# Load order at the start of a fused cross-attention and FFN kernel: three batches of x and context ahead of scales, zeros and packed weights, with one GpSimd reduction and one row maximum moved

## The reference, cut to what matters

```python
def xattn(up, down, Wq, Wk, Wv, Wskip):           # up = layernorm(x)
    q, k, v = Wq @ up, Wk @ down, Wv @ down        # per batch
    attention = softmax(q.T @ k / sqrt(128), axis=-1)      # 1024 x 256
    return Wskip @ up + v @ attention.T

x = x + xattn(layernorm(x), ctx, Wq, Wk, Wv, Wskip)
Wg, Wu, Wd = (dequantize(W_q, scale, zero) for gate, up, down)   # int4, groups of 64
n = layernorm(x)
x = x + (silu(n @ Wg.T) * (n @ Wu.T)) @ Wd.T      # 1024 -> 2752 -> 1024, 2048 tokens
```

## Time and profile before

| | us |
|---|---|
| median of 3 runs | 1503.36 |
| lowest and highest of them | 1502.53, 1504.96 |
| the profiled execution, its own time | 1508.22 |
| span of its instructions | 1506.3 |
| PE busy (share of the span) | 1456.6 (97%) |
| VectorE busy | 797.2 (53%) |
| ScalarE busy | 656.0 (44%) |
| GpSimd busy | 220.6 (15%) |
| mean granted TensorE clock, of full speed | 0.992 |

### The profile page before, as it was taken

How to read it: one execution, slowest core, us unless ns; L and a number is a source line. 1 busy time by engine, 2 the same in 40 slices (tenths; PEclk the granted TensorE clock), 3 DMA queues, 4 the chain that set the end, 5 groups by cost and what they waited for, 6 DMA issues and landing times.

```text
span 1506.3 us, 18670 instructions
## 1 busy us (share of the span) xinstructions
PE 1456.6 (97%) x6774; PEld 716.0 (48%) x6774; DVE 797.2 (53%) x1143; ACT 656.0 (44%) x1221; POOL 220.6 (15%) x281
## 2 busy tenths in 40 slices
PE   5999999999999999999999999999999999999995
PEld 4666665444444444444444444444444444444442
DVE  4788887745544544544544554553554554553330
ACT  4888884244244343333333433433433334334343
POOL 0223231011011111111111101101101101101112
PEclk8999999999999999999999999999999999999999
DMA  5222222157547647648638638638638637638739
GB/s 147 95 95 91 82 88 70 43 92 148 110 75 162 111 70 167 111 64 173 111 57 179 111 56 177 116 48 174 116 54 168 115 64 156 122 62 165 140 67 168
DMA packets 44723, 166.42 MB, mean 110 GB/s; under 512 B 6416, under 2 KB 9232, under 8 KB 40336
## 3 DMA queue, kind: packets, MB, share of 16 engines
q0 software_dynamic: 25344, 92.29, 37.1%
q1 hardware_dynamic: 19200, 73.42, 17.6%
q10 hardware_dynamic: 144, 0.26, 0.0%
HBM read 65.28 MB, written 100.66 MB: 110 GB/s over the span
## 4 chain that ended last, share of the span: by engine, by line
PE 88%; DVE 5%; issue 3%; ACT 2%; DMA 1%; POOL 0%; POOLq 0%; ACTq 0%; DVEq 0%
PE ps L487 47%; PE ps L543 26%; PE ps L449 3%; PE ps L416 3%; PE ps L444 2%; PE ps L633 2%; PE ps L438 2%; PE ps L404 1%; PE ps L648 1%; DVE w_gu L1106 1%; DVE neg_max L1029 1%; ACT stage L797 1%; DMA out<-stage 1%; ACT temps L686 1%; DVE quant L1122 0%
## 5 line engine op out<-in xcount | busy, mean ns | idle before, releaser
L487 PE MATMUL ps<-xt,w_gu 128*128 128x512 f16 x3528 | 790.9, 380 | 2.2 <-ACT temps L767 2.2
L487 PEld LDWEIGHTS ps<-xt,w_gu 128*128 128x128 f16 x3528 | 345.5, 98 | 418.6 <-ACT temps L767 3.0
L543 PE MATMUL ps<-w_d_all,h_all 128*128 128x512 f16 x1920 | 440.6, 379 | 5.6 <-ACT stage L797 5.6
L797 ACT ACTIVATE stage<-ps,pow 128x512 f32<-128x512 f32 x352 | 240.5, 687 | 407.1 <-PE ps L543 390.3
L364 POOL DMA_DIRECT2D out<-stage x176 | 152.4, 866 | 1098.4 <-ACT stage L797 1098.4
L543 PEld LDWEIGHTS ps<-w_d_all,h_all 128*128 128x128 f16 (+1 forms) x1920 | 187.2, 98 | 234.4 <-ACT stage L797 10.1
L1170 DVE TENSOR_TENSOR temps<-ps,temps 128x512 f32<-128x512 f32 x42 | 29.0, 692 | 237.7 <-PE ps L487 237.7
L784 ACT CAST h_all<-temps 128x512 f16<-128x512 f32 x42 | 25.8, 613 | 132.4 <-DVE temps L1189 132.4
L1175 DVE TENSOR_TENSOR temps<-ps,temps 128x512 f32<-128x512 f32 x42 | 29.0, 691 | 95.4 <-PE ps L487 95.4
L1179 DVE TENSOR_TENSOR temps<-ps,temps 128x512 f32<-128x512 f32 x42 | 28.9, 689 | 75.8 <-PE ps L487 75.8
L1183 DVE TENSOR_TENSOR temps<-ps,temps 128x512 f32<-128x512 f32 x42 | 28.9, 689 | 75.1 <-PE ps L487 75.1
(11 more groups left out here) (112 smaller groups left out, 1262.4 us busy)
## 6 DMA issues: line engine op xcount, KB each, us to landing
out<-stage POOLq DMA_DIRECT2D x176, 512.0 KB, 5.4
grid<-grids SPq DMA_DIRECT2D x136, 256.0 KB, 4.9
raw<-packed SPq DMA_DIRECT2D x22, 512.0 KB, 4.2
stage<-x SPq DMA_DIRECT2D x13, 512.0 KB, 3.9
out<-stage SPq DMA_DIRECT2D x13, 512.0 KB, 2.9
raw_d<-packed SPq DMA_DIRECT2D x12, 512.0 KB, 7.9
w_gu<-ctx SPq DMA_DIRECT2D x16, 128.0 KB, 2.0
w_gu<-x SPq DMA_DIRECT2D x3, 512.0 KB, 3.4
```

Of the source, the lines that this page charges most:

```text
L487: mm = pe.matmul(bank, w_gu[e][:, wp, w, P * j:P * j + P], xt[:, xb, xp, j, cols], start=(fresh and n == 0), stop=(n == 3 * J - 1), skip_g ...
L543: mm = pe.matmul(ps[:, 6 + oh, :], h, w, start=(n == 0), stop=(n == len(products) - 1))
L797: act.activation(stage[:, t % STAGES, NOUT * oh:NOUT * oh + NOUT], ps[:, 6 + oh, :], ACT.Copy, scale=pow2[:, 10:11]).then_inc(s_stage, 1)
```

## The change

Three moves, nothing is added or removed. On SyncE, x and context of the third batch (i = 2) are issued ahead of the six transfers of scales and zeros, and those of the fourth and fifth ahead of the packed weights and grid of job 0. On GpSimd, the reduction L346 moves behind the inverse deviation of batch 3 in step 1. On VectorE, the second maxima of batch 0 move ahead of the statistics of batch 2.

```diff
@@ SyncE
-            load_batch(0)
-            load_batch(1)
-            for k in range(3):
-                sp.dma_start(grids_all[:, k, :], scales[k, :, :]).then_inc(s_grids_in, 16)
-                sp.dma_start(grids_all[:, 3 + k, :], zeros[k, :, :]).then_inc(s_grids_in, 16)
-            load_raw(0, 0)
-            load_grid(0, 0)
-            for i in range(2, B):
+            for i in range(B):
                 load_batch(i)
+                if i == 2:
+                    for k in range(3):
+                        sp.dma_start(grids_all[:, k, :], scales[k, :, :]).then_inc(s_grids_in, 16)
+                        sp.dma_start(grids_all[:, 3 + k, :], zeros[k, :, :]).then_inc(s_grids_in, 16)
+                if i == 4:
+                    load_raw(0, 0)
+                    load_grid(0, 0)
                 if i >= 4:
                     store_batch(i - 4)
@@ GpSimd
             inverse_deviation(0, 2)
-            pool.wait_ge(s_extreme, 1)
-            pool.partition_all_reduce(pow2_tmp[:, 0:6], pow2[:, 0:6], P,
-                                      bass.bass_isa.ReduceOp.max).then_inc(s_extreme_all, 1)
             for i in range(1, STEPS):
...
                 if i + 2 < B:
                     inverse_deviation(0, i + 2)
+                if i == 1:
+                    pool.wait_ge(s_extreme, 1)
+                    pool.partition_all_reduce(pow2_tmp[:, 0:6], pow2[:, 0:6], P,
+                                              bass.bass_isa.ReduceOp.max).then_inc(s_extreme_all, 1)
                 if k >= 0:
@@ VectorE, step(i)
                 if i + 2 < B:
+                    if i == 0:
+                        maxima(0, 1)
                     x_arrived(i + 2)
                     row_stats(0, i + 2)
-                if i < B:
+                if 0 < i < B:
                     maxima(i, 1)
```

## The result

| | before | changed kernel |
|---|---|---|
| median of 11 runs, us | 1504.60 | 1508.45 |
| lowest and highest, us | 1502.53, 1508.40 | 1506.71, 1513.44 |
| profiled execution: own time, us | 1508.22 | 1513.44 |
| profiled execution: span, us | 1506.3 | 1509.8 |

The changed kernel is slower: ratio 1.0029, 95% interval 1.0019 to 1.0039, which is 3.85 us by the medians and 2.9 to 5.9 us by the interval. The forecast was 1507.6 us and +4.2 us. Both profiled executions are long ones of their kernels: 3.6 us above the median before, 5.0 us above it after.

The account below looks back on a forecast made before the run. The prediction saw a TensorE-bound chain (88%) with an early 6.05 us stall for x of batch 2. Lead left -0.99, clock +2.2 and slowed loading +3.0 gave +4.2 us, 1507.6 us; range 1501.5 to 1512.5.

Parts of the forecast that it names:

- Lead from loads and maxima: Step from batch 0's second maxima to batch 1's energies: second exponentials start at 17.48, not 24.54, 7.06 us earlier.
- The first low stretch stays, shifted.: TensorE's first stretch at the lower clock, 1.2 GHz, was expected to remain, only moved in time.
- The gap: 13.2 us whatever the inputs do: GpSimd, from the power ahead of the reduction to the next add: 13.2 us, leaving 0.99 of the 7.06 us lead.
- the list of signs: Expected trace marks, among them VectorE waiting some 7 us for `rstd` ahead of `normalize(1, 0)` and TensorE idle from about 40.7.
- Clock: +2.2 us: TensorE after idling 6.2 us in 6.9 before `keys_values(3)`: the clock falls to the lower level, costing 2.2 us.
- Loading under traffic: +3 us: GpSimd's code loads around the reduction, slowed by batch 4, raw and grid transfers: +3 us, bounds nothing to +12.8.
- Faster: GpSimd is free in time: Rival at `rstd` of layer norm 1, batch 0: whole 7.06 us lead stays, no pause, 1496.3 us; chance 0.07.
- Loading is not slowed: Rival on GpSimd's code loads: traffic adds nothing, -0.99 + 2.2 = +1.2 us, 1504.6 us; chance 0.27.
- The clock stays up: Rival on TensorE's pause: no lower clock, +2.0 or -1.0 us, 1505.4 or 1502.4 us; chance 0.08.

Follow-up runs that it names:

- no code needed: Changed kernel with the GpSimd reduction over partitions replaced by an ordinary add of the six maxima to themselves, same place and waits: 1500.34 us, ratio 0.9961.
- the one with the pause filled: Changed kernel with 28 extra identity products on TensorE in step 2, ahead of the block that waits for normalize(1, 0): 1507.33 us, ratio 1.0010.

## Why the prediction was right, step by step

**Lead from loads and maxima: 7.06 us forecast.** The second exponentials came at 17.1 and not at 24.54, 7.5 us earlier by the two profiles. Half a microsecond of it is that everything began at 5.36 instead of 5.83 us there, so 7.0 us are the change's. x of batch 2 was issued at 8.65 and landed 3.3 us later, as taken from the later x. The six maxima found their data at 17.85. Over the whole kernel less of it arrives: 5.1 to 6.2 us in the three measurements in which nothing took the lead back (reduction in its old place, twice, and no code needed), 5.4 with the loads alone and 4.2 with the maxima alone. The intervals of the first three reach up to 7.2 to 8.3 us, so 7.06 isn't excluded.

**"The first low stretch stays, shifted."** It came earlier and was shorter. In windows of 2 us the granted clock is down from about 18.6 to 32.3 us before, from 16.6 to 23.4 after and from 16.8 to 20.3 in the second profile of the changed kernel. So the power ahead of the reduction ended at 29.47 and 28.30 us, forecast 30.19: a further lead of 0.7 and 1.9 us that the forecast did not have.

**The gap: 13.2 us whatever the inputs do.** Confirmed, with scatter upward: 13.0 to 14.9 us in all thirteen profiles with the reduction, and no gap where no other code was needed. `normalize(1, 0)` came at 45.25, forecast 44.28 without traffic. The lead at `inverse_total(2, 0)` was 0.02 us, forecast 0.99 less the 3 us of slowed loading. The wait in the list of signs ("some 7 us") is that of the rival without slowdown, from the end of the first maxima near 37 to 44.28; with the 3 us of the forecast it would have been some 10. Measured were 9.45 us, from 35.8 to 45.25, and 8.53 in the second profile.

**Clock: +2.2 us.** Measured 9.10 - 6.85 = 2.25 us, and undone by filling the pause. In the other four profiles with the pause unfilled the stretch takes 8.5 to 9.1 us, so the price is 1.7 to 2.3.

**Loading under traffic: +3 us.** This term was mis-sized. The gap grew by 1.7 us in the first profile, 0.9 in the second and 0.4 in the one with the pause filled, and even its cause is not settled: a kernel without raw and grid beside the loads had a gap 0.9 longer too. Nor does any queue show the load as a transfer: from 24.3 to 30 us, over the whole first load of the kernel before, not one packet was moved.

**Sum.** By the first pair of profiles it is -0.02 + 2.25 = +2.2 us at 57.6 us, where the prediction has -0.99 + 2.2 + 3.0 = +4.2; of the 2.0 us between them 0.7 are the further lead and 1.3 the loading. The second profile of the changed kernel has keys and maxima of batch 3 here:

```profile
46.58 1.19 PE ps L393 x2
...
55.08 1.24 DVE neg_max L1030
```

That is 0.3 us ahead of the kernel before (55.38) and not 2.2 behind it. So one pair of profiles does not carry the sum, and the medians say +3.85, with 2.9 as the lower end of the interval. The mechanism is shown, by the runs with the reduction back and with no other code. That the number came so near is partly luck: a loading term that was too large stood in for 1.6 us and more that the first 60 us do not show. The clock stretches farther back, -1.7 us at 267 us and +3.0 at 1474 us in the first pair, are of that size, and neither is in the prediction. What the missing part is made of in the medians is not shown.

**The rivals.** "Faster: GpSimd is free in time" needed the gap under 5.8 us; it never was under 13. "Loading is not slowed", 1504.6 us, is not refuted as a mechanism, since traffic's part is open, but its +1.2 us lies below the measured interval. "The clock stays up" is out by the windows. The change is one useful part (loads, with the maxima worth little beside them) and one harmful part, and the harmful part was larger.

## What to carry to other kernels

The cross-partition reduction on GpSimd cost the time of two loads on that engine, here 13 to 15 us, most of it outside its own record: look in the queue's records for configuration changes on both sides, and in the timeline for the "issue" waits behind them, and put such an instruction where the next result of that engine is that far away. The record alone is no proof of a wait. The instruction at L315 of the kernel before has a pair too and starts at 1.50 us:

```profile
L315 POOLq MODIFY_POOL_CONFIG  x2: 11/14/16, 1.4 to 1.4; - x2
```

A shift of the work around it moves the place where the loads are hidden, so that it has to be placed anew when something ahead becomes faster. And a wait on a light engine that empties TensorE, here for 4.1 to 6.4 us, is paid a second time by the lower clock behind it.

## What had not been expected of the hardware

The first load does not wait for the input of the reduction. In the kernel with the six maxima moved it began at 19.70, ahead of the maxima (19.84 to 22.41), and the reduction still came 5.74 us later, as soon as in kernels whose maxima were long done (5.8 to 7.4 us in those with the reduction moved). The Trainium skill, GPSIMD Engine Reference, section 2.1 Instruction dispatch, gives about 6 us for a first call of loaded code; here each of the two took between 5.6 and 7.9 us, and either of them could be the longer-than-usual one. And the gain of a busy pause stopped at the next engine: with energies up to 1.8 us shorter, the value products started 1.0 us later than they could have.
